# Expert rows rounded up to 32 in place of 128 in the second expert layer, with mixed blocks in column tiles

## What is computed

```
shared = silu(xt @ Wg_s) * (xt @ Wu_s) @ Wd_s
probs = sigmoid(xt @ W_router + routing_bias)
scores, idx = top_k(probs, 2);  scores = scores / sum(scores)
g = einsum('th,ehi->tei', xt, Wg_r);  u = einsum('th,ehi->tei', xt, Wu_r)
combined = einsum('tei,eih,te->th', silu(g) * u, Wd_r, wts)
out = shared + combined
```

## Time and profile before

| | us |
|---|---|
| median of 3 runs | 1744.53 (1744.31 to 1749.68) |
| profiled execution, its own time | 1747.71 |
| span of that execution | 1745.8 |
| TensorE busy | 1526.1 (87%) |
| DVE busy | 955.3 (55%) |
| ACT busy | 486.1 (28%) |
| POOL busy | 490.2 (28%) |
| mean granted TensorE clock | 0.944 of full |
| shared expert and routing of the second expert layer | about 948 to 997 |
| its expert blocks | about 997 to 1120 |

### The profile page before, as it was taken

One profiled execution on the slowest core, in us unless ns is written; L12 is line 12 of the kernel. 1 busy time (PEld: TensorE's weight loads), 2 busy tenths in 40 slices (PEclk: granted clock), 3 DMA queues, 4 the chain that ended last, 5 costly groups with the idle time before them and its releaser, 6 DMA issues. The chain is left out here.

```text
span 1745.8 us, 33514 instructions
## 1 busy us (share of the span) xinstructions
PE 1526.1 (87%) x11918; PEld 1150.5 (66%) x11919; DVE 955.3 (55%) x2460; ACT 486.1 (28%) x1027; POOL 490.2 (28%) x597
## 2 busy tenths in 40 slices
PE   4887899999979979699997999767888788899995
PEld 3664799999958843355544566445665665599995
DVE  4556244444448957666636533469888465522221
ACT  2331111011047731265542122233332333011110
POOL 0102344444410001111112144333212010366663
PEclk9998899999979999799998999888899899999998
DMA  4109677677620005433403333210000003688885
GB/s 142 44 2 308 193 218 231 211 222 229 195 58 2 2 1 139 115 106 104 107 16 103 104 82 85 82 49 19 7 1 1 1 2 98 220 239 240 239 238 148
DMA packets 128625, 200.84 MB, mean 115 GB/s; under 512 B 20352, under 2 KB 77952, under 8 KB 128320
## 3 DMA queue, kind: packets, MB, share of 16 engines
q1 hardware_dynamic: 107680, 169.65, 30.5%
q0 software_dynamic: 20832, 29.68, 8.1%
HBM read 166.21 MB, written 35.16 MB: 115 GB/s over the span
## 5 line engine op out<-in xcount | busy, mean ns | idle before, releaser
L1541 DVE TENSOR_REDUCE l1a_nm<-l1a_sc 128x1 f32<-128x512 f32 (+3 forms) x256 | 107.2, 483 | 52.8 <-PE l1a_sc L1677 52.8
L2354 ACT ACTIVATE e0b_sg<-e0b_gp 128x640 f32<-128x640 f32 x78 | 33.5, 481 | 267.2 <-PE e0b_gp L2294 267.2
L2267 POOL DMA_INDIRECT y_sum<-e0b_yb,e_token x39 | 63.2, 1620 | 140.3 <-DVE e0b_yb L2381 137.4
L2267 POOL DMA_INDIRECT y_sum<-e3b_yb,e_token x39 | 62.7, 1608 | 61.0 <-DVE e3b_yb L2381 56.1
L2354 ACT ACTIVATE e3b_sg<-e3b_gp 128x512 f32<-128x512 f32 x39 | 23.3, 598 | 189.3 <-PE e3b_gp L2294 189.3
L1675 PE MATMUL l1a_sc<-l_stack_k,l_stack_q 128*128 128x512 bf16 (+3 forms) x256 | 59.6, 311 | 16.3 <-PEq L1323 15.0
L2461 PE MATMUL e1b_gu<-e_kgu,e1b_xT 128*128 x152 | 71.7, 594 | 1.7 <-DVE e1b_xT L2525 1.7
L2373 DVE TENSOR_TENSOR e0b_hT<-e0b_up,e0b_sg 128x640 f32<-128x640 f32 x39 | 32.2, 825 | 70.6 <-PE e0b_up L2294 59.3
L1675 PEld LDWEIGHTS l1a_sc<-l_stack_k,l_stack_q 128*128 128x128 bf16 x256 | 25.4, 99 | 60.6 <-issue 26.9
L1430 POOL TENSOR_TENSOR xn<-xn 128x512 f32<-128x512 f32 x8 | 10.1, 1262 | 194.9 <-DVE xn L1385 183.4
L2617 POOL TENSOR_TENSOR f_hq<-f_q,f_q 128x704 f32<-128x704 f32 x16 | 22.9, 1433 | 137.2 <-DVE f_q L2604 137.2
(11 more groups left out here) (633 smaller groups left out, 4086.6 us busy)
## 6 DMA issues: line engine op xcount, KB each, us to landing
e3k_wgu<-in_L_ffn_W SPq DMA_DIRECT2D x40, 512.0 KB
e3b_wgu<-in_L_ffn_W SPq DMA_DIRECT2D x38, 512.0 KB
e0k_wgu<-in_L_ffn_gate_proj SPq DMA_DIRECT2D x20, 704.0 KB
e0k_wgu<-in_L_ffn_up_proj SPq DMA_DIRECT2D x20, 704.0 KB
e0b_wgu<-in_L_ffn_gate_proj SPq DMA_DIRECT2D x19, 704.0 KB
e0b_wgu<-in_L_ffn_up_proj SPq DMA_DIRECT2D x19, 704.0 KB
x_rows<-xn SPq DMA_DIRECT2D x3, 2048.0 KB, 9.6
l_parts<-l1p_split SPq DMA_DIRECT2D x16, 384.0 KB, 3.1
```

What stands on the lines that cost most here:

```text
L1541: nc.vector.tensor_reduce(nm[:, g % 2, q, i:i + 1], sc[q], AX_X, ALU.max, negate=True).then_inc(max_done, 1)
L2267: pool.indirect_dma_start(y_sum, bass.IndirectOffsetOnAxis(ap=token[:, n:n + 1], axis=0), yb[n % 2][:], None, compute_op=ALU.add).then_inc ...
L2354: last = nc.scalar.activation(sg[rows, chunks, :], gp[rows, chunks, :], ACT.Silu)
```

## The change

An expert's tokens are laid out in units of 32 rows in place of 128. For each expert, its whole groups of 128 rows go to whole blocks; what is left, rounded up to 32, is one to three quarters. Quarters fill mixed blocks, each of four quarters with up to four owners. The counts are fixed for any routing by the new class `Layout`: with 7 experts and units of 32 it gives 28 whole blocks and 6 mixed ones, 34 in all, in place of 38, and 28 + 24 = 52 owners in place of 38.

- The order of work is not the order in DRAM: `order()` puts a mixed block behind each 4 or 5 whole ones. In the order of work the mixed blocks are at places 4, 10, 16, 21, 27 and 33, the last being the last block.
- A mixed block's gate/up and down products are four matmuls of 32 stationary columns for each chunk in place of one of 128, each writing 32 partitions of the same PSUM bank.
- A mixed block's weights aren't taken from the kept copies. SP reads the four owners and loads their gate, up and down matrices from DRAM into `mixed_gu` and `mixed_d` (12 transfers of 256 KB), of which there is one set. The first load is issued at the start of the stage; each later one behind the write of the mixed block before, thus once `y_copied` has counted that block. TensorE waits for all 12 (`mixed_in`) ahead of the mixed block's gate/up product.
- In `route`, the 6 instructions on DVE from `cnt` to `base` become 15 with shifts and masks, `past` grows from 38 x 6 to 52 x 13, and `owner` takes two instructions in place of one.
- The constants gain a row of 52 numbers; two semaphores are new.

The core of the diff:

```diff
+class Layout:
+    def __init__(self, experts, unit):
+        self.experts, self.unit, self.per = experts, unit, P // unit
+        most = (TOP * B * S + experts * (unit - 1)) // unit
...
+    def order(self):
+
+        return [b for i in range(self.mixed) for b in
+                (*range(i * self.full // self.mixed, (i + 1) * self.full // self.mixed), self.full + i)]
+
+    def owner_at(self, n):
+        return [n] if n < self.full else [self.full + (n - self.full) * self.per + u for u in range(self.per)]
...
+QUARTERS = Layout(NE - 1, P // 4)
...
-                NB = (TOP * B * S + E * (P - 1)) // P
+                lay = QUARTERS
+                NB = lay.blocks
...
+                        bits = lay.unit.bit_length() - 1
+                        nc.vector.tensor_scalar(held_i[:], count, float(lay.unit - 1), None, ALU.add).then_inc(laid, 1)
+                        dve.wait_ge(laid, 1)
+                        nc.vector.tensor_scalar(parts_i[:, 0, :], held_i[:], P.bit_length() - 1, None, ALU.logical_shift_right)\
+                            .then_inc(laid, 1)
...
+                        nc.vector.tensor_tensor(past[:], bcast(const("quarters"), 2, 2 * E - 1), bcast(begins[:, 1:], 1, lay.owners),
+                                                ALU.is_ge).then_inc(step, 1)
...
+                        nc.vector.tensor_scalar(wrap[:], own[:], float(E), -float(E), ALU.is_ge, ALU.mult).then_inc(laid, 1)
+                        dve.wait_ge(laid, 15)
+                        nc.vector.tensor_tensor(owner[:, 0:lay.owners], own[:], wrap[:], ALU.add).then_inc(step, 1)
...
+            mixed_gu, mixed_d = tmp("mixed_gu", [P, PER, KC, 2 * F]), tmp("mixed_d", [P, PER, FC, D])
+            mixed_in, MIXED_IN = sem("mixed_in"), 16 * 3 * PER
...
+                    def load_mixed(n):
+
+                        for u, at in enumerate(lay.owner_at(order[n])):
+                            e = sp.value_load(owner[0:1, at:at + 1], min_val=0, max_val=experts_n - 1)
+                            for to, m in ((mixed_gu[:, u, :, 0:F], weights[0]), (mixed_gu[:, u, :, F:], weights[1]), (mixed_d[:, u], weights[2])):
+                                sp.dma_start(to, m[e].rearrange("(k p) f -> p k f", p=P)).then_inc(mixed_in, 16)
+
+                    load_mixed(mixed_at[0])
                     for n in range(NB):
                         sp.wait_ge(y_copied, n + 1)
-                        sp.dma_start(y_slots.rearrange("(n p) d -> n p d", p=P)[n], yb[n % 2][:]).then_inc(rows_out[n % 2], 16)
+                        sp.dma_start(y_slots.rearrange("(n p) d -> n p d", p=P)[order[n]], yb[n % 2][:]).then_inc(rows_out[n % 2], 16)
+                        if n in mixed_at[:-1]:
+                            load_mixed(mixed_at[mixed_at.index(n) + 1])
...
+                        if is_mixed(n):
+                            pe.wait_ge(mixed_in, MIXED_IN * (mixed_at.index(n) + 1))
                         for k in range(KC):
-                            last = nc.tensor.matmul(gu[n % 2][:], xT[n % 2][:, k, :],
-                                                    wgu[:, bass.ds(e, 1), k, :].rearrange("p a f -> p (a f)"),
-                                                    start=(k == 0), stop=(k == KC - 1))
+                            if is_mixed(n):
+                                for rows, u in side_by_side():
+                                    last = nc.tensor.matmul(gu[n % 2][rows, :], xT[n % 2][:, k, rows], mixed_gu[:, u, k, :],
+                                                            start=(k == 0), stop=(k == KC - 1))
```

## The result

The changed kernel takes 1781.62 us (median, 1774.09 to 1793.6) beside 1746.47 for the kernel before (four runs of each): ratio 1.0206, 95% interval [1.0146, 1.0266]. Its profiled execution has a span of 1779.1 us, 33.3 more than before's 1745.8, and a mean granted clock of 0.94.

What follows compares the result with a forecast made beforehand. TensorE, working through the whole expert-block stretch at 2.4 GHz, was taken as the bound. Terms -12.1 + 3.0 + 28.5 + 11 + 1 + 0.5 = +31.9 us gave 1779.6 profiled, 1776 on the median; range 1756 to 1803.

Steps and rivals of the forecast that it cites:

- the rivals: Refetch hidden, 1737 us; faster fetch, short waits, 1749; column tiles one after another, 1820: 0.05 each; clock holds, 1765, within forecast.
- four blocks fewer: Expert-block stage: 38 blocks become 34, each worth 3.02 us on TensorE's path, 12.1 us less.
- narrow products: Mixed blocks' gate/up and down products: four narrow ones run at once, 0.5 us more a block, 3.0 us for six.
- waits at five refetches: TensorE before later mixed blocks: waits of 5.2 us four times and 7.7 us once, 28.5 us; bounds 18 to 51.
- clock: TensorE behind each refetch wait: clock falls to 1.2 GHz, five times 2.2 us, 11 us; bounds 0 to 15.
- start of the stage: First fetch is hidden but shares the engines with block 0's gather: 1 us, from 0 to 2.
- routing: DVE's longer chain and larger past table: 3.5 us, hidden behind TensorE's shared expert; 0.5 us, from 0 to 3.5.
- one step of 3.5: Expected sign in the profile after: mixed blocks' narrow products with 3.5 us from block to block.
- the fetch starts at T + 1.15: SP's refetch starts 1.15 us after T, the start of the gate/up product three blocks after a mixed one.
- Size of the fetch: Refetch of 3.15 MB: 9.0 us at 348 GB/s, 2.0 latency, 2.1 for gathers and a write; 13.1 us.
- The write behind the fetch: Block m+1's write queues behind the fetch: costs nothing while TensorE waits; without that cover about 3 us a refetch.
- The larger constants: The larger constants, priced together with the two new semaphores: 0 us.

Runs made afterwards that it cites:

- busy: Changed kernel with TensorE multiplying constants into an unused PSUM bank before each wait for refetched weights, 26 products (38 at the short step): 1777.5 us, ratio 1.0175.
- half: Changed kernel fetching only two of the four experts again at each refetch, so part of the output is wrong: 1750.96 us (one run).
- spread: Changed kernel fetching all mixed weights in pieces as buffer parts come free, down with its own semaphore, first fetch behind the first gather: 1735.9 us, ratio 0.9937.
- consts: Kernel before with only the added row of 52 constants, which nothing reads: 1737.92 us, ratio 0.9948.
- spread2: As spread, but at the short step gate and up weights are fetched two experts at a time: 1732.33 us, ratio 0.9919.
- hoist: Changed kernel with SP reading the next four owners before its wait for the mixed block's results, not between transfers: 1779.36 us, ratio 1.0192.
- once: Changed kernel without the five later fetches; later mixed blocks reuse the first one's weights, so part of the output is wrong: 1739.21 us, ratio 0.9949.

## Why the prediction was right, and where its terms were off

The forecast was 1776 within 1756 to 1803, with TensorE waiting at each refetch and its clock falling; that is what happened. None of the rivals did: no fetch was hidden or short, the narrow products ran side by side, and the clock fell behind each of the five waits. But the total agrees better than its terms.

| term | forecast | measured |
|---|---|---|
| four blocks fewer | -12.1 | -12.1 |
| narrow products | +3.0 | +3.7 |
| waits at five refetches | +28.5 | +36.1 |
| clock | +11 | about +12 |
| start of the stage | +1 | +4.0 |
| routing | +0.5 | 0 |
| sum of these rows | +31.9 | +43.7 (the stage itself +43.3) |
| everything ahead of the stage | 0 | -9.7 (one pair of profiles; medians -9) |

- **Narrow products.** 16 records of gate/up run for 1.86 us (1008.70 to 1010.56 in after) where a wide product has 1.72, and the four steps around a mixed block are 3.11, 3.21, 3.25 and 3.12 in place of 3.02: 0.6 us a mixed block against 0.5, and spread over four steps, not one step of 3.5. The Trainium skill's figure for column tiles ("TensorE: Matmul & The Clock Gate", Part 3), by which I had estimated 0.68 us, lies a little above the measured 0.61, mine a little more below.
- **Waits: right in kind, 7.6 us too small.** 51.64 us of steps less five of 3.11 are 36.1 (the profile books 34.3 of it as idle). The step "the fetch starts at T + 1.15" failed: it starts at T + 2.36 (1020.54 - 1018.18). 0.6 of the difference is the copy of the mixed block's results, which begins at T + 0.83 (1019.01) where before's begins at T + 0.20; 0.6 is the first reading of an owner, 0.76 us for the 0.15 I had put there. Five times 1.2 are 6.0 us. The other 1.6 are the fetch itself, 13.5 us on average for 13.1 (12.6 at the short step), less 0.2 us for the longer steps of 3.02 to 3.12 us that hide it.
- **Size of the fetch.** The rate taken from the earlier trace rows was right for the part behind SP's last issue, 346 GB/s; while SP issues it was 320, gathers included, and the whole took 0.4 us longer than forecast. The Trainium skill's formula ("DMA: Bandwidth & Descriptors", Anatomy of one DMA), 9.2 us by my estimate, is 4.3 us short of the measured 13.5 for these 1 KB rows, with the gathers beside them. The page fits it to single transfers on the gpsimd path; here 12 are issued by SP.
- **The clock.** 2.1 to 2.8 us at half speed behind each wait, for 2.2; `busy` shows it apart. `half` adds that its four short waits (1.2 to 1.5 us idle) cost nothing of it here.
- **The write behind the fetch: nothing, as forecast.** In `busy`, where the clock holds, the steps behind a fetch are 3.02 to 3.25 us.
- **The start.** I priced only the sharing, 1 us. The gather's wait grew by 2.4 us, as 12 transfers stand beside it, and the clock fell behind it as well, 1.5 us more on the next step. In `spread`, where the first fetch stands behind that gather, the wait is 1.43 and the next step 2.80.
- **Routing.** DVE's longer chain stayed behind TensorE's shared expert, as the earlier trace rows had it: no wait appeared, and the stretch is 0.9 us shorter with the faster loads.
- **The larger constants: 0.** This is the step that failed outright. They moved every tile behind them, and with that 1 KB transfers went from 349 to 386 GB/s; which waits ahead of the stage became shorter by it was not taken apart. Measured at equal places, after against `consts`, the change costs 1781.6 - 1737.9 = 43.7 us, and the stage accounts for all of it (173.3 - 130.1 = 43.2).

So the mechanism and the range held, but that the total came within 6 us of 1776 is luck: the error of the stage (11 us too little) was covered by a gain of some 9 that I hadn't seen.

## What to carry to other kernels

A refetch into a single buffer costs what its issue time and bytes leave over the steps that hide it, plus the clock behind each long wait: price the issue from the instruction that frees the buffer, with the register reads ahead of each transfer, and release the buffer in parts as each consumer is done. The same bytes, placed so, cost 1.8 us of waiting in place of 34.3. And where a change adds or grows a tile near the start of SBUF, compare the parts that it doesn't touch, and judge it against the kernel before with the same shift: `spread2` is 14 us faster than the kernel before, but only 5.6 us faster than `consts` (their intervals still touch), and some 8 are the shift (`consts`).

## What the runs showed of the hardware that I had not expected

- Transfers with 1 KB rows between DRAM and SBUF ran at 343 to 349 GB/s where the tile started 32 to 384 bytes past a multiple of 512 in its partition, and at 385 to 387 where it started on one (371 to 385 for inner in after); in this kernel that is 9 us of 1746. A multiple of 256 or of 1024 isn't told apart from 512 by these runs.
- SP needs about 0.6 us to read one number from SBUF into a register between two transfers: the gap between the transfers of two experts is 0.75 us or more in after and 0.18 to 0.20 in `hoist`, where the numbers are read ahead.
- The results of narrow column tiles came to DVE later: the copy begins 0.63 us later after the same product's start than behind a wide one (T + 0.83 for T + 0.20). In `once`, without any refetch, it is T + 0.85.
